# Two layers on one core: two of an expert's four lower products made from rounded halves

## The reference, cut to what matters

```python
x = x + a
gates = jax.nn.softmax(x @ Wg + bg, axis=-1)
hmid = jax.nn.relu(jnp.einsum('bsh,ehd->bsed', x, W1) + b1)
eout = jnp.einsum('bsed,edh->bseh', hmid, W2) + b2
y = jnp.einsum('bse,bseh->bsh', gates, eout)
return x + y
```

## Time and profile before

| | |
|---|---|
| median of 3 runs | 1013.37 us (1011.25 to 1015.28) |
| profiled execution | 1019.3 us, of which the span of the trace is 1017.5 us |
| PE busy | 936.2 us (92%) |
| DVE, ACT, POOL busy | 608.9, 567.8, 347.9 us (60%, 56%, 34%) |
| mean granted TensorE clock | 0.963 of full speed |

### The profile page before, as it was taken

One profiled execution on the slowest core, in us unless ns is written; L12 is line 12 of the kernel. 1 busy time (PEld: TensorE's weight loads), 2 busy tenths in 40 slices (PEclk: granted clock), 3 DMA queues, 4 the chain that ended last, 5 costly groups with the idle time before them and its releaser, 6 DMA issues.

```text
span 1017.5 us, 17056 instructions
## 1 busy us (share of the span) xinstructions
PE 936.2 (92%) x6324; PEld 628.5 (62%) x6324; DVE 608.9 (60%) x1747; ACT 567.8 (56%) x965; POOL 347.9 (34%) x436
## 2 busy tenths in 40 slices
PE   4599889888988999999999999999999998988997
PEld 3355555545656787656666566666666666877983
DVE  8988778577475675355554535554455764747334
ACT  4477876775774565445465455545555565453430
POOL 4446540330000000233424443243533323457671
PEclk9599999989997999999999999999999998998999
DMA  5865342643593000101101111111101213112316
GB/s 136 205 156 133 101 122 66 157 123 141 123 226 125 23 22 3 43 21 52 53 22 63 42 40 44 47 37 42 62 21 53 73 47 97 44 50 72 107 46 227
DMA packets 86398, 83.10 MB, mean 82 GB/s; under 512 B 9202, under 2 KB 72680, under 8 KB 86316
## 3 DMA queue, kind: packets, MB, share of 16 engines
q1 hardware_dynamic: 81092, 73.32, 26.1%
q0 software_dynamic: 4320, 8.27, 2.5%
q10 hardware_dynamic: 904, 0.42, 0.1%
HBM read 50.53 MB, written 31.72 MB: 81 GB/s over the span
## 4 chain that ended last, share of the span: by engine, by line
PE 56%; DVE 13%; issue 10%; ACT 9%; SPq 5%; POOL 5%; DMA 2%; another core or an unknown queue 0%; POOLq 0%; DVEq 0%; ACTq 0%
PE psum L1454 13%; PE psum L1487 12%; PE psum L1477 4%; PE psum L1309 4%; PE psum L1247 3%; PE psum L1263 2%; PE psum L1290 2%; POOL routed L2691 2%; SPq L1091 2%; ACT ew L2323 1%; PE psum L1217 1%; PE psum L1239 1%; POOL hT L2633 1%; DVE maxes L1844 1%; PE psum L1368 1%
## 5 line engine op out<-in xcount | busy, mean ns | idle before, releaser
L2432 ACT ACTIVATE big<-psum,cols 128x512 f32<-128x512 f32 x256 | 173.8, 689 | 162.7 <-PE psum L1454 152.1
L1454 PE MATMUL psum<-parts,q_stack 128*128 128x512 f32 x640 | 260.2, 488 | 4.2 <-issue 2.3
L1487 PE MATMUL psum<-big,ew 128*128 128x512 f32 x512 | 249.5, 595 | 0.0
L2633 POOL TENSOR_TENSOR hT<-hT,gb_tok 128x512 f32<-128x512 f32 x56 | 73.6, 1315 | 289.5 <-DVE gb_tok L1965 289.1
L1454 PEld LDWEIGHTS psum<-parts,q_stack 128*128 128x128 f32 x640 | 113.4, 194 | 61.7 <-issue 50.1
L1844 DVE TENSOR_REDUCE maxes<-psum 128x4 f32<-128x1024 f32 (+1 forms) x96 | 114.8, 1218 | 27.6 <-PE psum L1263 27.3
L1487 PEld LDWEIGHTS psum<-big,ew 128*128 128x128 f32 x512 | 96.1, 190 | 53.2 <-issue 39.9
L1454 PE MATMUL psum<-parts,k_stack 128*128 128x512 f32 x320 | 127.5, 398 | 0.0
L1965 DVE SCALAR_TENSOR_TENSOR gb_tok<-psum,cols,gb_tok 128x512 f32<-128x512 f32 x64 | 47.9, 749 | 92.4 <-PE psum L1487 84.7
L2714 POOL DMA_INDIRECT answers<-hT,to x64 | 62.5, 976 | 54.7 <-DVE hT L2163 38.0
L2691 POOL DMA_INDIRECT routed<-big,slot_i x64 | 63.2, 988 | 41.8 <-DVE slot_i L2143 22.2
(11 more groups left out here) (401 smaller groups left out, 1656.2 us busy)
## 6 DMA issues: line engine op xcount, KB each, us to landing
gb_tok<-gate_rows SPq DMA_DIRECT2D x32, 512.0 KB
q_stack<-q_pieces SPq DMA_DIRECT2D x32, 192.0 KB, 3.5
k_stack<-k_pieces SPq DMA_DIRECT2D x32, 192.0 KB, 4.5
routed<-empty_row SPq DMA_DIRECT2D x4, 1040.0 KB, 13.4
big<-routed SPq DMA_DIRECT2D x16, 260.0 KB
answers<-gb_tok SPq DMA_DIRECT2D x4, 1024.0 KB, 11.1
q_pieces<-gb_tok SPq DMA_DIRECT2D x16, 192.0 KB, 2.1
k_pieces<-gb_tok SPq DMA_DIRECT2D x15, 192.0 KB, 2.1
```

The source lines that it names most:

```text
L1454: last = eng.matmul(bank(i), w1_part(wp, e)[:, fs], parts[2 * xk + xp][:, :], start=n == 0, stop=n == 2)
L1487: eng.matmul(bank(i), ew2[:, e, f, :], hid[:, r, f, :], start=f == 0, stop=f == FC - 1).then_inc(sem("down", "pe"))
L2432: eng.activation(hid[:, held("hid", "up", n, e, f), f, :], bank(held("bank", "up", n, e, f)), ACT.Relu, bias=col("L0_ffn_b1", e * FC + f)) ...
L2633: eng.tensor_tensor(hT[:, ns], xpT[:, ns] if e == 0 else hT[:, ns], gate_wide[:, e // GHELD % 2, e % GHELD, :], ALU.add).then_inc(sem("acc ...
```

## The change

In chunks 0 to 6 (`cut_in_two`: `n < NCH - 1 and f in SPLIT`), the lower products f = 1 and f = 3 are made the way the upper ones are: three f32r matmuls of split operands. That adds a step `hs(n, e, f)`, in which ACT copies the relu tile to an f32r piece and DVE subtracts this from the tile into a second piece (7 x 8 x 2 = 112 times), and a step `sv(e)`, which splits the two weight blocks of expert e into `w2_parts` (8 times). The lower products f = 0 and 2, and all of chunk 7, stay float32.

The storage changes with it. Instead of two `hid` buffers of four tiles each, a relu tile takes one of five single `slot`s. It is free after the float32 `down`, or, for a split one, after `hs` on DVE. Pieces have two pairs in `big2` and, once the weights of layer 1 have been turned (`wt(4)`), a third. `w2_parts` lies over `ew1`, so `w1`, the load of layer 1's weights, waits for the last split lower products of chunk 6. `hid` comes into being for the routed experts when those places are free again.

In the diff, the first `hs` function is that of DVE, the second that of ACT. The declared durations and the ranks change too: `up` pe .75 act .6 becomes pe .765 act .72, and `down(e, f)` now ranks behind `up` three places further on (`AHEAD = 3`), where before it ranked behind all four `up` of the next expert.

```diff
+SPLIT = (1, 3)
+AHEAD = 3
+def cut_in_two(n, f):
+
+    return n < NCH - 1 and f in SPLIT
...
-    p.pool("hid", range(2))
+    p.pool("hid", ())
+    p.pool("slot", range(5))
+    p.pool("pieces", range(2))
...
-                p.step("up", n, e, f, work="pe:.75 act:.6", after=[("sx", n), ("sw", 0, e), last_pv]
...
-                p.step("down", n, e, f, work="pe:.88", after=[("up", n, e, f)]
...
+                rank, above, slot = at + 25 * f, p.buffer("bank"), p.buffer("slot")
+                p.step("up", n, e, f, work="pe:.765 act:.72", after=[("sx", n), ("sw", 0, e), last_pv]
...
+                if cut_in_two(n, f):
+                    pieces = p.buffer("pieces")
+                    p.step("hs", n, e, f, work="act:.62 dve:.72", after=[("up", n, e, f)], opens=[(0, pieces)],
+                           closes=[(1, slot)], slot=slot, pieces=pieces)
+                    p.step("down", n, e, f, work="pe:.69", after=[("hs", n, e, f), ("sv", e), *order], rank=rank + 25 * AHEAD + 12,
+                           opens=[(0, bank)] if f == 0 else [], closes=[(0, pieces)], bank=bank, pieces=pieces)
+                else:
+                    p.step("down", n, e, f, work="pe:.88", after=[("up", n, e, f), *order], rank=rank + 25 * AHEAD + 12,
+                           opens=[(0, bank)] if f == 0 else [], closes=[(0, slot)], bank=bank, slot=slot)
...
-    p.step("w1", work="sp:.1 dma:12", after=[("sw", 0, e) for e in range(NE)])
+    for e in range(NE):
+        p.step("sv", e, work="act:.42 dve:.45", after=[("sw", 0, e), ("bg", 2), ("bg", 3)]
+               + ([(("up", 0, e - 1, 0), "pe")] if e else []))
...
+    p.step("w1", work="sp:.1 dma:12", after=[("down", NCH - 2, e, SPLIT[-1]) for e in range(NE)])
...
             def down(n, e, f):
...
+                if cut_in_two(n, f):
+                    k, kx = held("pieces", "down", n, e, f), SPLIT.index(f)
+                    w.wait_ge(*done("hs", n, e, f))
+                    w.wait_ge(*done("sv", e))
+                    for m, (wp, xp) in enumerate(((0, 0), (0, 1), (1, 0))):
+                        last = eng.matmul(bank(i), w2_parts[:, e, wp, kx, :], halves[2 * k + xp][:, :],
+                                          start=f == 0 and m == 0, stop=f == FC - 1 and m == 2)
...
+            def hs(n, e, f):
+                k = held("pieces", "hs", n, e, f)
+                w.wait_ge(*done("hs", n, e, f, by="act"))
+                for c in cleared("pieces", "hs", n, e, f):
+                    w.wait_ge(*c)
+                eng.tensor_tensor(halves[2 * k + 1][:, :], slots[held("slot", "hs", n, e, f)], halves[2 * k][:, :].bitcast(F32),
+                                  ALU.subtract).then_inc(sem("hs"), 1)
...
+            def hs(n, e, f):
+                w.wait_ge(*done("up", n, e, f))
+                for c in cleared("pieces", "hs", n, e, f):
+                    w.wait_ge(*c)
+                eng.copy(halves[2 * held("pieces", "hs", n, e, f)][:, :], slots[held("slot", "hs", n, e, f)]).then_inc(sem("hs", "act"), 1)
```

More of the change, by code:

```diff
@@ L147 @@
     "sw": ("split", "act dve"), "sx": ("split", "act dve"),
-    "up": ("up", "pe act"), "down": ("down", "pe"), "mix": ("down", "dve"), "acc": ("down", "pool"),
+    "up": ("up", "pe act"), "hs": ("hidden", "act dve"), "sv": ("split", "act dve"), "down": ("down", "pe"), "mix": ("down", "dve"), "acc": ("down", "pool"),
     "sg_r": ("spread", "act"), "sg_m": ("spread", "pe act"),
@@ L595, in order_steps @@
[L595 to L599 removed]
+                rank, above, slot = at + 25 * f, p.buffer("bank"), p.buffer("slot")
+                p.step("up", n, e, f, work="pe:.765 act:.72", after=[("sx", n), ("sw", 0, e), last_pv]
+                       + ([(("up", n, e, f - 1), "pe")] if f else []), rank=rank, opens=[(0, above), (0, slot)],
+                       closes=[(1, above)] + ([(0, split)] if (e, f) == (NE - 1, FC - 1) else []), bank=above, slot=slot, parts=split)
@@ new lines, in order_steps @@
+                order = [("bg", 2), ("bg", 3)] + ([("down", n, e, f - 1)] if f else [])
+                if cut_in_two(n, f):
[7 more added lines that the diff above has]
+                           opens=[(0, bank)] if f == 0 else [], closes=[(0, slot)], bank=bank, slot=slot)
@@ L603, in order_steps @@
         add_mixed(n, MOE - 300, (20 + n, -1, 0))
-    p.step("w1", work="sp:.1 dma:12", after=[("sw", 0, e) for e in range(NE)])
+    for e in range(NE):
+        p.step("sv", e, work="act:.42 dve:.45", after=[("sw", 0, e), ("bg", 2), ("bg", 3)]
+               + ([(("up", 0, e - 1, 0), "pe")] if e else []))
+    third = [("wt", 4), last_pv]
+    p.step("third_over", after=third, then=found("pieces", (2,), ((("wt", 4), "pe"), (last_pv, "pe"))))
+    p.step("w1", work="sp:.1 dma:12", after=[("down", NCH - 2, e, SPLIT[-1]) for e in range(NE)])
+    for half, pool, ids, last in ((1, "pieces", (0, 1), [("down", NCH - 2, e, f) for e in range(NE) for f in SPLIT]),
+                                  (0, "slot", range(4), [("down", NCH - 1, e, f) for e in range(NE) for f in range(FC)])):
+        old = [p.buffer(pool, i) for i in ids]
+        p.step("free", "hid", half, work="sp:0", after=last, opens=[(0, b) for b in old],
+               then=lambda now, half=half, old=old: p.pools["hid"].update({half: sum((b.before for b in old), ())}))
     for e in range(NE):
```

53 lines of the change are left out of this document (35 added, 18 removed).

## The result

The changed kernel takes 1015.55 us (median of 20 runs, 1010.75 to 1020.12) against 1011.67 us (1005.61 to 1015.28) for the kernel before on the same chips. The ratio is 1.0042, 95% interval 1.0026 to 1.0059: 4 us slower, where 16.5 us faster was forecast. The predicted 997 us and its range up to 1012 us both miss. (The prediction counts from 1013.4, the median of the three executions known when it was made.)

A forecast was written before the change was run, and what follows sets the result against it. PE's work alone was taken to set the pace from about 340 to 847 us. Products -18.5, w1 -3 and new waits +5 made 16.5 us less: 1013.4 to 996.9, predicted 997 us, range 984 to 1012, forecast's own 990 to 1005.

The forecast's parts named there:

- What bounds the kernel now: From about 340 to 847 us PE alone sets the pace; a microsecond off its work there is one off the kernel.
- Part 1, the products: Chunks 0 to 6: 112 split lower products at 0.69 us in place of 0.857, saving 18.5 us.
- Part 2, w1: Near 312 us: moving layer 1's weight load lets the first gates land sooner, saving 3 us, bounds 0 and 5.8.
- The bound of 5.8: Near 312 us: most the moved load can give back, 2.6 us of waits plus 3.2 us lost to the clock.
- Part 3, ACT and DVE: Chunks 0 to 6: hs adds 68 us to ACT and 77 to DVE; neither becomes the bound, but lateness can cost.
- for new waits of PE I take 5 us: Seven chunks 0 to 6: PE waits 0.7 us more in each, 5 us together, bounds 0 and 20.
- a block of 1.1 us fits into 1.4 us of slack alone: Between up and split down: a subtraction delayed 1.1 us by POOL is covered by slack, but not together with a queue.
- three in ten: Chunks 0 to 6: perhaps this share of the 112 hs subtractions meets a POOL operation, POOL being busy 37%.
- Part 4, the rest: Slots, ranks and the reordered plan change no work; nothing counted, 3 us allowed either way for the reordering.
- Operands come late: Rival, chunks 0 to 6: PE's in-order wait for hs makes the kernel slower, 1020 to 1049 us; slower than 1018: 0.08.
- Another engine or the chain of layer 1 becomes the bound: Rival: existing PE waits of 9.1 us double, giving 1001 us, within the forecast's range; no chance of its own.
- four signs of being wrong: PE waits for pieces over 20 us; split matmuls further apart than up's; subtraction mean over 0.9 us; clock under 1.00.

The follow-up runs named there:

- g1: Kernel before, same order, lower products 1 and 2 of chunk 7 over 128 of 512 columns; ratio to before 1.0007.
- g2: Kernel before, same order, lower products 1 and 2 of chunks 0 to 6 over 412 of 512 columns; ratio to before 0.9887.
- g3: Changed kernel with all lower products float32, no hs or sv, lower products 1 and 2 of chunks 0 to 6 over 412 of 512 columns; ratio to before 0.9963.
- g6: Changed kernel, same order, hs copy and subtraction both over 128 of 512 columns, split products reading a weight block instead; ratio to before 0.9792.
- e4: Kernel before with only the load of layer 1's weights delayed until chunk 6's last lower product; ratio to before 1.0006.
- its twin: Kernel before run unchanged again for a second trace; ratio to before 1.0001, span 1015.3 us.
- e2: Changed kernel, split products reading a weight block and waiting for the relu alone, all pieces still made, another order; ratio to before 0.996.
- f2: Changed kernel with AHEAD = 4 in place of 3, another order; ratio to before 1.0106.
- e5: Changed kernel with the hs subtraction reading the product from its PSUM bank instead of the SBUF relu tile, another order; ratio to before 0.993.
- g4: Changed kernel, same order, hs subtraction on DVE over 128 of 512 columns, split products reading a weight block instead; ratio to before 0.9815.
- g5: Changed kernel, same order, ACT's hs copy over 128 of 512 columns, subtraction full, split products reading a weight block instead; ratio to before 0.9997.
- e8: Kernel before with only up's declared durations changed (PE .75 to .765, ACT .6 to .72), so another order; ratio to before 1.0071.
- e6: Changed kernel with the subtraction reading PSUM and the relu writing the rounded piece, so no ACT copy; ratio to before 0.9856.
- f3: Changed kernel with relu writing the rounded piece, subtraction reading PSUM, and lower products 0 and 2 split instead of 1 and 3; ratio to before 0.9857.
- f1: Changed kernel with DVE's part of hs declared to the planner at .85 us in place of .72; ratio to before 1.007.

## Why the prediction was wrong, point by point

**What bounds the kernel now: wrong, and the root of it.** "PE alone sets the pace from about 340 to 847 us" was concluded from a busy share of 98%. g1 shows that less work for PE in chunk 7 gains nothing: the way of chunk 6 through `acc`, linear attention, routing and fetch (59.1 us from the last `acc` to the first fetch) ends 3.3 us after PE's products, and PE had merely no more to do. g2 shows that in chunks 0 to 6 of that order some 60% of a saving on PE is passed on; the rest turns into waits for layer 1's steps on DVE, ACT and POOL. The share is a matter of the order: g3 passes on half, while g6, the changed kernel without the work of `hs`, is 21 us faster than the kernel before. A busy PE beside three engines at 37 to 53% can still be paced by them, when their operations form one chain that must come back to PE in order.

**Part 1, the products: right.** 0.70 us on the chain for a split product, against the forecast 0.69.

**Part 2, w1: right near 320 us, nothing as a whole.** 3 us were forecast; e4 has 4.7 in A, 2.1 lost in B, and a ratio of 1.0006. (The bound of 5.8 counts PE's 2.6 idle us twice. The clock took 0.32 of the 7.38 busy us, 2.4 in place of 3.2, so 5.0 together.) Part of the stall was a peculiarity of the first trace, as its twin shows.

**Part 3, ACT and DVE: the step that failed.** The term "for new waits of PE I take 5 us", bounds 0 and 20, measured 25 us with the order fixed (g6 against the changed kernel): 21 to 23 for the subtraction, 2 to 5 for the copy. The miss of the whole forecast, 20 us, is this term's. The busy times were right (ACT 72% and DVE 71% were forecast; 68% and 70% of 400 us came out). What was wrong was to let a load cost something, in the main, through PE's wait for its own result, with 1.4 us of slack as the cover. Of the idle time that g6 takes from PE, that wait is 4 us in 15.5; e2 took it away altogether and f2 almost, in other orders, and both left chunks 1 to 6 as long as they were. The rest are waits for layer 1's steps, whose DVE operations share a queue with the subtractions; that this queue is the way is read from those waits.

The port conflict was seen in the right row. It was argued from it that "a block of 1.1 us fits into 1.4 us of slack alone". It met 18 of the 112 subtractions and not three in ten, but it is not confined to the product that waits: the mean of POOL's line 2747 is 1.56 us in place of the 1.27 to 1.29 of an undisturbed one. e5, which takes the second SBUF input away, is 11 us faster than the changed kernel, but its order is not the same, and an order alone was worth 7 us. Nor are the 11 us a share of the 21 to 23: e5 takes away DVE's waits for POOL, which g4 leaves as they are. The price of the conflict stays open.

The rule of the Trainium skill that the prediction weighed (SBUF — State Buffer, the reading of its diagram: VectorE with two SBUF inputs against a GpSimd operation that reads SBUF, exclusively and for the whole instruction) is borne out here: 18 subtractions with two SBUF inputs are lengthened, each beside POOL, and none of e5's 112 once one input comes from PSUM.

**Part 4, the rest: right in the sum, wrong in its parts.** "The last 167 us hold the same work. I allow 3 us either way for the reordering" was too narrow for any one place. B is 79.3 us in place of 69.4, and g4, g5 and g6 keep it at 78.1 to 79.4 whatever is done to `hs`. So these 10 us belong to the frame and its order, not to the new operations. e8 gives a measure of what an order alone does: 7 us. Most of the 10 us lie in layer 1's chain for chunk 6: from the last `acc` of chunk 6 to the fetch it takes 66.6 us in the changed kernel (65.9 to 66.6 in g4 to g6) and 59.1 before. In the changed kernel DVE takes up the top-2 choice of chunk 5 only at 778.7 us, 3.8 us after that `acc` has started; before, POOL starts chunk 5's fetches 8 us ahead of it. So layer 1's chain for chunk 5 is late and runs into that for chunk 6. That this is the mechanism of the 10 us is argued from the trace, no run isolates it.

**The account**, in us against the kernel before: -21 for the changed kernel without the work of `hs` (g6), +25 for that work, together +4 as measured. The forecast had -21.5 (products 18.5, w1 3) and +5. That the first pair agrees is partly luck. In g6, B is 9 us longer; the products' 18.7 (a calculation, not isolated in this order) and w1's 4.7 would leave -15, and the other 6 us are a gain of the new order in A, which no run explains.

**The rivals.** "Operands come late" had the right sign and priced a loss of 28.5 us at 1020 us, but its mechanism, PE's wait for `hs`, is the smaller part of the loss. "Another engine or the chain of layer 1 becomes the bound" was the nearest, and I had left it at 9 us because no engine came near 100%.

**The signs.** Of the four signs of being wrong none showed clearly: PE itself waited 9.5 us for the pieces (over 20 only with the weight load's waits, 29.6), the split products are as far apart as the upper ones, the subtraction's mean is 0.85 us, the clock 1.00. What did show it was the chunks' period, 61.7 us in place of the forecast 58 to 59, and PE idle for 5.4% in place of under 4%.

**What stays open:** the division of the loss between shared port and mere occupancy, the 6 us that the new order gains in A, and which misplaced steps make stretch B long.

## What to carry to other kernels

When a change takes work from the busiest engine and gives more to others (here 19 us less for one and 68 and 77 us more for two), test first whether the saving is passed on: shorten the operation by the intended amount, leave everything else in place, and read the ratio. In a kernel whose order is computed from declared durations, compare only variants with a fixed order, or take the spread between orders (7 us here) as the error of every comparison. And try to split a tile where it leaves PSUM: with the relu writing the rounded piece and the subtraction reading the bank, the same idea was 1.4% faster than the kernel before (e6, f3). These kernels are not finished ones: their subtraction leaves out the bias, and no run shows what it costs to put it back.

## What the runs showed of the hardware

- A DVE operation with two SBUF inputs of 128 x 512 takes 0.68 us, and up to 2.64 us in the changed kernel, beside POOL's additions and multiplications on SBUF. Between chunk 1 and chunk 6, 28 to 36 POOL operations were over 0.2 us longer than the shortest of their form in the kernels that subtract 512 columns from SBUF (the changed kernel, e2, f1, f2, g5), 11 in e5 and e6, 9 in the kernel before, 9 with the subtraction cut to 128 columns (g4, g6).
- The short subtraction waits for POOL as the long one does: 0.28 us alone, up to 2.80 us in g4 and 2.85 in g6.
- DVE's scaling on line 1828, with one SBUF tensor and two per-partition scalars as inputs, takes 0.34 us and up to 1.33 us. All 13 that were over 0.2 us longer in the changed kernel overlap POOL's `acc`; in the kernel before (second trace) there were 5.
- The same subtraction with one input from PSUM takes 0.684 us, no more than from SBUF, and less than the 0.75 us that I had expected from `mix`.
